# KDA block: both kinds of decay-scaled rows in one tile, made by one GpSimd instruction per level

## The reference

```
state = state * exp(g_i)[..., None]
inner = einsum('bhk,bhkv->bhv', k_i, state)
state = state + einsum('bhk,bhv->bhkv', b_i[..., None] * k_i, v_i - inner)
o_i   = einsum('bhk,bhkv->bhv', q_i, state)
```

## Time and profile before

| what | value |
|---|---|
| median of 3 runs | 7801.84 us (7801.79 to 7804.72) |
| profiled execution, its own time | 7796.2 us |
| its span, first to last instruction | 7794.4 us |
| PE busy | 6437.2 us, 83% |
| DVE busy | 3340.8 us, 43% |
| ACT busy | 2901.9 us, 37% |
| POOL busy | 2502.6 us, 32% |
| mean granted TensorE clock | 0.859 of full speed |

### The profile page before, as it was taken

One profiled execution on the slowest core, in us unless ns is written; L12 is line 12 of the kernel. 1 busy time (PEld: TensorE's weight loads), 2 busy tenths in 40 slices (PEclk: granted clock), 3 DMA queues, 4 the chain that ended last, 5 costly groups with the idle time before them and its releaser, 6 DMA issues. The chain is left out here.

```text
span 7794.4 us, 119680 instructions
## 1 busy us (share of the span) xinstructions
PE 6437.2 (83%) x49476; PEld 4302.2 (55%) x49476; DVE 3340.8 (43%) x4774; ACT 2901.9 (37%) x5214; POOL 2502.6 (32%) x1697
## 2 busy tenths in 40 slices
PE   6787788798755889688888888888888999888999
PEld 5666666466543666355556556555564444665444
DVE  4333333333324233356566565565553113565121
ACT  2121111334333343354554544545453113666111
POOL 3334443100001000255656556565562221000222
PEclk8777778787876878798989889889898999888999
DMA  0000000000000000000000000000002110001111
GB/s 22 0 0 0 0 0 0 26 0 0 12 0 26 0 0 1 18 18 15 14 20 14 14 20 14 19 15 14 20 14 78 42 34 32 0 0 57 42 42 46
DMA packets 60088, 134.58 MB, mean 17 GB/s; under 512 B 11414, under 2 KB 23702, under 8 KB 58490
## 3 DMA queue, kind: packets, MB, share of 16 engines
q1 hardware_dynamic: 59770, 129.66, 5.1%
HBM read 127.13 MB, written 2.50 MB: 17 GB/s over the span
## 5 line engine op out<-in xcount | busy, mean ns | idle before, releaser
L569 PE MATMUL ps<-moe_xn_all,moe_w 128*128 128x512 f32 x1792 | 808.3, 594 | 1.6 <-DVE moe_h L682 1.6
L569 PEld LDWEIGHTS ps<-moe_xn_all,moe_w 128*128 128x128 f32 x1792 | 340.1, 191 | 424.6 <-issue 421.7
L1694 PE MATMUL ps<-kda_xn_all,kda_w_front 128*128 128x512 f32 x808 | 463.0, 726 | 128.9 <-ACT kda_cv L1733 103.7
L1983 POOL TENSOR_TENSOR kda_g<-kda_g,kda_f 128x512 f32<-128x512 f32 x225 | 423.0, 1880 | 455.9 <-DVE kda_rows L1975 447.8
L682 DVE TENSOR_TENSOR moe_h<-moe_silu,ps 128x512 f32<-128x512 f32 x224 | 153.9, 687 | 935.8 <-ACT moe_silu L624 928.7
L1806 DVE SCALAR_TENSOR_TENSOR kda_cv<-kda_pre,kda_w_front,kda_cv 128x1024 f32<-128x1024 f32 x297 | 551.5, 1857 | 3.6
L624 ACT ACTIVATE moe_silu<-ps 128x512 f32<-128x512 f32 x224 | 133.8, 597 | 986.0 <-PE ps L569 985.9
L525 POOL TENSOR_TENSOR moe_h<-moe_h,moe_cb 128x512 f32<-128x512 f32 x176 | 234.0, 1330 | 696.0 <-DVE moe_h L682 696.0
L579 PE MATMUL ps<-moe_h,moe_w 128*128 128x512 f32 x896 | 420.4, 592 | 0.0
L1975 POOL TENSOR_TENSOR kda_rows<-kda_q,kda_f 128x512 f32<-128x512 f32 x225 | 322.7, 1434 | 241.3 <-remote 212.0
L1694 PEld LDWEIGHTS ps<-kda_xn_all,kda_w_front 128*128 128x128 f32 x808 | 178.4, 232 | 344.9 <-issue 199.4
(11 more groups left out here) (489 smaller groups left out, 14464.2 us busy)
## 6 DMA issues: line engine op xcount, KB each, us to landing
kda_col<-kda_beta SPq DMA_DIRECT2D x34, 512.0 KB, 4.1
moe_w<-in_Mw SPq DMA_DIRECT2D x6, 2816.0 KB, 20.6
moe_cb<-kda_beta SPq DMA_DIRECT2D x64, 256.0 KB, 3.2
kda_w_front<-in_Kw SPq DMA_DIRECT2D x34, 455.0 KB, 4.7
moe_cb<-kda_beta SPq DMA_DIRECT2D x32, 224.0 KB, 2.9
kda_w_out<-in_Kw SPq DMA_DIRECT2D x32, 192.5 KB, 4.7
moe_cb<-kda_beta SPq DMA_DIRECT2D x32, 192.0 KB, 2.8
moe_cb<-kda_beta SPq DMA_DIRECT2D x32, 160.0 KB, 2.7
```

Source lines behind the costliest of these rows:

```text
L569: last = nc.tensor.matmul(ps_gu[u % 2][r], w13[:, k, i, r], n.xn[:, k, cols(c)], start=k == 0, stop=k == KD - 1)
L1694: last = nc.tensor.matmul(psum(g, FRONT + hf, BANK), w[:, at:at + P], xn_all[:, k, bass.ds(quad * QUAD + hf * BANK, BANK)], start=k == 0, ...
L1983: step(nc.gpsimd.tensor_tensor(halves(decay_g[:], h, 0), halves(decay_g[:], h, 0), second_total, ALU.mult))
```

## The change

The q and a tiles become two halves of one tile, `rows`, of [128, 2, 4, 256], with a in the first and q in the second. `scale_rows` loses its engine and kind arguments: it is one GpSimd multiplication of 1024 elements in a partition, over both halves, with `o.f` read twice through a step of zero. DVE's six `a_rows` per block go away, with their waits. In `first_rows` two GpSimd instructions become one. The semaphore `rows_scaled` is now raised by GpSimd's rows, and `scaled` by the columns alone, so the counts waited for become l in place of 2 * l.

```diff
-        ops = [Names(q=s.sb(f"q{i}", wide), a=s.sb(f"a{i}", wide), f=s.sb(f"f{i}", wide), col=s.sb(f"col{i}", wide),
+        ops = [Names(rows=s.sb(f"aq_rows{i}", [P, 2, UNITS, SEQ]), f=s.sb(f"f{i}", wide), col=s.sb(f"col{i}", wide),
                      v=s.sb(f"vt{i}", [P, QT, UNITS, P])) for i in range(2)]
+        for o in ops:
+            o.a, o.q = o.rows[:, 0], o.rows[:, 1]
...
-        def scale_rows(engine, o, l, r, done):
+        def scale_rows(o, l, done):
+
             h = 1 << l
-            out = rows_s[l % 2][:, r].rearrange("p u (b h) -> p (u b) h", h=h)
-            engine.tensor_tensor(out, halves((o.a, o.q)[r][:], h, 1), halves(o.f[:], h, 1), ALU.mult).then_inc(done, 1)
+            out = rows_s[l % 2][:].rearrange("p r u (b h) -> p r (u b) h", h=h)
+            src = o.rows[:].rearrange("p r u (b two h) -> p r (u b) two h", two=2, h=h)[:, :, :, 1]
+            f = halves(o.f[:], h, 1).unsqueeze(1).to_broadcast([P, 2, UNITS * SEQ // (2 * h), h])
+            nc.gpsimd.tensor_tensor(out, src, f, ALU.mult).then_inc(done, 1)
...
             pool.wait_ge(m.rows_ready, 2)
-            for r in range(2):
-                scale_rows(nc.gpsimd, o, 0, r, n.first_scaled)
+            scale_rows(o, 0, n.first_scaled)
             pool.wait_ge(n.g_clear, 1)
-            pool.wait_ge(n.first_scaled, 2)
+            pool.wait_ge(n.first_scaled, 1)
...
-                scale_rows(nc.gpsimd, cur, l, 1, n.scaled)
+                scale_rows(cur, l, n.rows_scaled)
                 nc.gpsimd.tensor_tensor(halves(cols_s[l % 2][:], h, 0), halves(cur.col[:], h, 0),
                                         halves(decay_g[:], h, 0), ALU.mult).then_inc(n.scaled, 1)
-                pool.wait_ge(n.scaled, 2 * l)
+                pool.wait_ge(n.scaled, l)
                 pool.wait_ge(n.rows_scaled, l)
...
-            def a_rows(l):
-                if l >= 2:
-                    dve.wait_ge(n.g_step, 2 * (l - 1))
-                    dve.wait_ge(n.sc_ready, l - 1)
-                scale_rows(nc.vector, o, l, 0, n.rows_scaled)
...
-            a_rows(1)
             for j in range(CONV - 1):
                 f.tap(0, j)
...
             masks(1)
-            a_rows(2)
             f.tap(1, 0)
...
```

More of the change, by code:

```diff
@@ L2023, in scores @@
             def scores(l):
-                pe.wait_ge(n.scaled, 2 * l)
+                pe.wait_ge(n.scaled, l)
                 pe.wait_ge(n.rows_scaled, l)
@@ L2039, in last_scores @@
             def last_scores():
-                pe.wait_ge(n.scaled, 2 * B_LEVELS)
+                pe.wait_ge(n.scaled, B_LEVELS)
                 pe.wait_ge(n.rows_scaled, B_LEVELS)
@@ L2259, in chain_dve @@
             masks(2)
-            a_rows(3)
             f.tap(1, 2)
@@ L2264, in chain_dve @@
             masks(3)
-            a_rows(4)
             f.tap(2, 0)
@@ L2271, in chain_dve @@
             masks(4)
-            a_rows(5)
             f.corr(0)
@@ L2276, in chain_dve @@
             masks(5)
-            a_rows(6)
             update(5)
```

## The result

The changed kernel takes 7840.36 us (median of 5 runs, 7830.43 to 7845.74) against 7801.84 (5 runs, 7799.81 to 7804.72): a ratio of 1.0048, 95% interval 1.0033 to 1.0063. It is slower by 38.5 us, and 7840 had been forecast. The profiled execution has 7845.74 us beside a span of 7844.0.

What follows compares the result with a forecast made beforehand. It took each block as a chain through PE and DVE, with GpSimd off it; delays at line 1879 of 13.7, 18.4 and 6.6 sum to 38.7 us, added to the 7801.8 median: 7840.5, forecast 7840, range 7772 to 7868.

Steps and rivals of the forecast that it cites:

- The instruction's price: Combined GpSimd instruction: 2.83 us at levels 0 and 1, 2.35 above; bounds 1.9 and 2.54.
- The start: Start of a block: GpSimd first, third tap ends at 8.77 us against 8.89 before, `lt_times_t(0)` 0.1 earlier.
- DVE goes first: Rival at a block's start: first tap precedes GpSimd's rows, 25 blocks gain 1.4 us, 7 lose 0.95; -28, 7774; chance 0.13.
- the state: State matmuls at line 1879, timed from a block's start: forecast 15.64 us, or 16.10 where PE starts late.
- the 7 blocks: First block of each loop iteration after the first, PE starting late: line 1879 from 15.15 to 16.10, 0.95 us later.
- Level 2 and clip: At level 2 GpSimd's rows hold line 2247 (2.5 us, not 1.53), its columns hold `f.clip` (1.7, not 0.68); chance 0.50.
- Clip is free: Rival at level 2: `f.clip` isn't held by GpSimd, only 7 blocks lose 0.9 us each; +6, 7808; chance 0.19.
- The sum: Delay of line 1879 summed over 32 blocks: 38.7 us, with nothing downstream giving it back.
- the table: Delay of line 1879 by kind: 7 blocks by 1.95 us (13.7), 18 by 1.02 (18.4), 7 by 0.95 (6.6).
- The count of 7, 18 and 7 blocks: Blocks sorted by line 1879's start before the change: 7 at 13.69 us, 18 at 14.62, 7 at 15.15.
- Two places lose: Rival: clip stands and level 5's rows precede `tap(2, 0)`, delaying `update(3)` some 1.0 us a block; 71, 7873; chance 0.08.
- GpSimd becomes the bound: Rival: GpSimd's load binds; needs over 5 us a block, six levels add 6.6 but lose waits; chance next to nothing.

Runs made afterwards that it cites:

- Experiment 5: The changed kernel, with GpSimd waiting at level 1 until DVE's first tap of the block is done; 7749.01 us, ratio 0.9922-0.995.
- experiment 8: The changed kernel, with each level's rows made by two GpSimd instructions of 512 elements in place of one of 1024; 7694.07 us, ratio 0.9867-0.9897.
- Experiment 4: The changed kernel, with GpSimd waiting at level 2 until clip is done; 7800.23 us, ratio 0.9989-1.0011.

## Why the prediction was right, point by point

**The instruction's price.** 2.81 measured at level 1 for 2.83, and above it 2.35 to 2.39 for 2.35 where nothing holds it (levels 2, 4 and 6 of the block shown): it costs 0.19 less than twice 1.27, and far more than the 1.9 of the lower bound.

**The start.** Taps to 8.77 forecast, 8.78 measured; `lt_times_t(0)` 9.75 (mean), 0.14 earlier than before, for 0.1. GpSimd was first, as forecast. Experiment 5 shows what the rival *DVE goes first* would have done: the state at 12.73 and, in the 7 blocks, at 16.06, for which 16.10 had been said. Its mechanism was right and its price of 28 us too low: 54 were measured. Left out was PE's clock: the half-clock stretch about 10 to 13 us into a block, worth up to 0.8 us in `lt_times_t(0)` alone (1.97 in the earlier trace rows, 1.15 here), is there in all of the changed kernel's 24 blocks and gone from 18 of these (from 22 in experiment 8).

**Level 2 and clip.** Addition 2.49 for 2.5, clip 1.76 for 1.76, state 15.56 for 15.64, and 16.13 for 16.10 in the 7 blocks. Experiment 4 takes both holds away and with them the loss. *Clip is free* is refuted by 32 instances of 1.65 to 1.76.

**The sum.** 38.7 forecast, 34.1 in the 31 blocks of the profiles (27.5 in the changed kernel's second profile), 38.5 and 34.9 between the medians. Between the first two profiles the mean shift of the state is 1.07 us a block, 33 in 31 blocks, and the rest nearly cancels: 0.22 more from the state to line 1890, 0.19 less from there to the block's end. PE waits for d in 26 blocks, not in 32: in the other 6 the granted clock is half from 8.5 to 15.3 us, and PE is itself as late.

That the total came out so close is in part luck. By length, the 24 blocks lose 0.75 us each (82.12 to 82.87), 18 us, where the table has 32 for its 25; the 7 lose 2.32 each (81.43 to 83.75), 16 us, where it has 6.6. The two second profiles give 0.64 and 2.01. So the shift at the state was forecast well, but it isn't passed on as it is: about 0.35 us is given back behind it in each of the 24, and 1.35 us are added behind it in each of the 7. The sentence that nothing downstream gives this back didn't hold, and what makes up the difference in the 7 stays open.

**The count of 7, 18 and 7 blocks.** The 18 blocks with 14.62 and the 7 with 13.69 had been read from single instances; 3 of the 18 start their state at 15.5 to 15.6, and could lose next to nothing there. Which kind a block is goes with PE's granted clock: in the 7 it isn't half between 9.5 and 14 us, in most of the 18 it is half from 9.8 to 13.2, in the 3 from 8.5 to 15.3. The second profile of the kernel before has the state at 15.50 in its 24 blocks and makes the time good later: the granted clock is half from about 8.5 to 15.3 us in all but the first of them, and full in their first 3 us, while the block is as long (81.91 and 81.97). The place of one matmul is therefore no measure of the loss between such executions; the length of the block is.

***Two places lose* and *GpSimd becomes the bound*.** `update(3)` starts at 37.13 for 37.1 forecast if the tap is ahead of level 5: it was. Experiment 8 settles the other.

What stays open is why the kernel before itself has two times, 7779 to 7786 and 7800 to 7812, with both in one group of runs. Its second profile (7804.5) is of the longer kind; the first (7796.2) lies between the two, nearer the longer, and none is of the shorter. The changed kernel's 11 runs all lie between 7830 and 7846.

## What to carry to other kernels

Where GpSimd and DVE take turns at SBUF, what an instruction costs is how long it keeps the other engine standing just when the chain needs that one: cut GpSimd's work into short instructions, since each gap can let DVE in, and look at which instruction of DVE is issued behind it. Moving work off a busy engine buys nothing if its other instructions then stand for as long; sum busy times before and after by line. Compare the length of the repeated block, since stages that the change doesn't touch moved by 12 us between two profiles of one kernel and by up to 24 between kernels. And check a loss by the kinds of blocks, not by its total alone.

## What the runs showed of the hardware

- A DVE `tensor_scalar` of 1024 elements from SBUF to SBUF, 0.68 us by itself, stands behind a GpSimd instruction: 1.75 us behind columns of level 2, 1.48 behind `decay_g` and 1.52 behind `o.f` in the blocks shown. It ends 0.53 to 0.56 us after the holder does, so once let in it takes no longer than by itself.
- An addition of PSUM and SBUF and a copy out of PSUM on DVE are not held: 0.69 us each, begun beside a GpSimd instruction of 2.36.
- A GpSimd multiplication with one input repeated by a step of zero costs nearly as much as two halves, 2.35 us for 1024 elements against twice 1.27 (2.54); at an inner run of 2 elements it costs 2.81, against twice 1.50.
- PE's clock is part of what a hold on DVE costs. Over 32 blocks the matmuls of `lt_times_t(0)` kept PE busy for 50.8 us in the kernel before and for 38.3 in experiment 8, where the wait ahead of them fell from 56.9 to 25.7; the mean granted clock over the loop was 0.90 and 0.93. The mean alone proves little: the second profile of the kernel before has 0.92 with blocks as long, and 98.2 us of that wait.
- The clock also differs in a layer that no edit touched: attention took 628 us at a granted 0.86 in the kernel before and 611 at 0.89 in experiment 8.
